# Masked query features written by four exponentials with their own bias columns

## What is computed

```python
h = _layernorm(x) * (1 + ca) + sa
x = x + ga * forward(h, ...)        # 3 layers, 16 heads of 8 channels
# in each layer
q, k, v = (out @ W + b  for Wq, Wk, Wv), split into heads
u = einsum(x * dh**-0.25, omega);  hh = 0.5 * sum(xs * xs)
favor(x) = concatenate([exp(u - hh), exp(-u - hh)]) * m**-0.5      # m = 8 features a head
a = causal_linear_attention(favor(q), favor(k), v) @ Wo + bo
h = layer_norm(out + a)
out = layer_norm(h + relu(h @ W1 + bf1) @ W2 + bf2)
```

## Time and profile before

| | us |
|---|---|
| median of 3 runs | 1801.07 |
| lowest and highest of them | 1798.61, 1804.36 |
| span of the profiled execution | 1828.0 |
| TensorE busy in it | 1571.7 |
| VectorE busy in it | 1443.5 |
| ScalarE busy in it | 935.3 |
| GpSimd busy in it | 698.6 |

### The profile page before, as it was taken

How to read it: one execution, slowest core, us unless ns; L and a number is a source line. 1 busy time by engine, 2 the same in 40 slices (tenths; PEclk the granted TensorE clock), 3 DMA queues, 4 the chain that set the end, 5 groups by cost and what they waited for, 6 DMA issues and landing times.

```text
span 1828.0 us, 65037 instructions
## 1 busy us (share of the span) xinstructions
PE 1571.7 (86%) x27934; PEld 1150.5 (63%) x27934; DVE 1443.5 (79%) x3906; ACT 935.3 (51%) x1958; POOL 698.6 (38%) x620
## 2 busy tenths in 40 slices
PE   6777365399969999999999999999999999999853
PEld 4344254399946677776667777666677667777542
DVE  4998566766658888888888888888888988888864
ACT  4887476366524444445544444554444544444373
POOL 0777636345513234215224323423321522431354
PEclk9888655599969999999999999999999999999876
DMA  9730012333200000000000000100000000000437
GB/s 264 145 100 1 21 50 90 97 102 101 83 13 14 3 9 9 15 3 14 15 3 13 16 3 8 20 3 9 9 15 3 14 15 3 11 6 3 109 102 233
DMA packets 88606, 79.69 MB, mean 44 GB/s; under 512 B 22416, under 2 KB 77040, under 8 KB 88064
## 3 DMA queue, kind: packets, MB, share of 16 engines
q1 hardware_dynamic: 70736, 46.17, 9.6%
q0 software_dynamic: 10848, 25.70, 4.9%
q10 hardware_dynamic: 6736, 3.66, 0.7%
HBM read 46.74 MB, written 34.01 MB: 44 GB/s over the span
## 4 chain that ended last, share of the span: by engine, by line
PE 50%; DVE 13%; ACT 4%; issue 2%; DMA 1%; DVEq 1%; POOL 0%; another core or an unknown queue 0%; POOLq 0%; ACTq 0%
PE psum L1965 8%; PE psum L1890 8%; PE psum L1859 4%; PE psum L1868 4%; PE psum L1928 2%; PE psum L1934 2%; PE psum L1882 2%; PE psum L1936 2%; PE psum L1875 2%; PE psum L1937 2%; PE psum L1938 2%; PE psum L1948 2%; PE psum L1847 2%; DVE at_kb L1543 2%; PE psum L1929 2%
## 5 line engine op out<-in xcount | busy, mean ns | idle before, releaser
L1890 PE MATMUL psum<-attn_w,at_qa 128*128 128x128 f32 x1536 | 197.6, 282 | 0.0
L1752 POOL TENSOR_TENSOR at_xres<-at_xn,attn_rows 128x512 f32<-128x512 f32 x32 | 40.9, 1277 | 394.2 <-DVE at_xn L368 394.2
L1965 PE MATMUL psum<-at_vT,attn_w 128*128 128x512 f32 x384 | 180.6, 614 | 6.8 <-ACT at_vT L1697 5.8
L1890 PEld LDWEIGHTS psum<-attn_w,at_qa 128*128 128x128 f32 x1536 | 179.6, 192 | 6.1 <-issue 0.7
L1543 DVE TENSOR_SCALAR at_kb<-at_kf,const 128x512 f32<-128x512 f32 x192 | 178.4, 989 | 0.0
L1757 POOL TENSOR_TENSOR at_xn<-at_sqk,attn_rows 128x512 f32<-128x512 f32 x48 | 63.6, 1326 | 202.8 <-DVE at_sqk L368 202.8
L1549 DVE STREAM_TRANSPOSE at_vb<-at_vT 32x512 uint32<-32x512 uint32 x192 | 134.7, 701 | 1.9
L1669 ACT ACTIVATE at_qa<-at_qf,const 128x512 f32<-128x512 f32 x192 | 127.6, 714 | 1.6
L1713 ACT ACTIVATE at_qa<-psum,attn_bf 128x512 f32<-128x512 f32 x192 | 122.1, 678 | 10.6 <-PE psum L1965 5.4
L1565 DVE TENSOR_TENSOR at_weights<-psum,const 128x1024 f32<-128x1024 f32 x96 | 115.6, 1204 | 11.3 <-PE psum L1859 11.3
L361 ACT ACTIVATE at_rstd<-at_mv,const 128x4 f32<-128x4 f32 x96 | 28.1, 292 | 184.3 <-DVE at_mv L349 184.2
(11 more groups left out here) (308 smaller groups left out, 3884.2 us busy)
## 6 DMA issues: line engine op xcount, KB each, us to landing
ex_rows<-sorted_x SPq DMA_DIRECT2D x71, 129.0 KB
ti_rows<-tile_rows SPq DMA_DIRECT2D x8, 640.0 KB
x<-in_L_attn_x SPq DMA_DIRECT2D x8, 512.0 KB, 7.3
tile_rows<-in_L_attn_x SPq DMA_DIRECT2D x8, 512.0 KB
x<-token_y POOLq DMA_DIRECT2D x8, 512.0 KB
tile_y<-ti_rows SPq DMA_DIRECT2D x16, 192.0 KB
out<-x ACTq DMA_DIRECT2D x12, 256.0 KB
expert_w<-in_L_ffn_w SPq DMA_DIRECT2D x1, 2048.0 KB, 14.2
```

Source lines behind the costliest of these rows:

```text
L1890: last = mm(bank(f.s, 1)[:, c * D:(c + 1) * D], hidden[f.s][:, t, c * P:(c + 1) * P], k.w2[:, f.l, t, :], start=(t == 0 and c == 0), stop= ...
L1965: mm(bank(f.s, c), k.w1[:, f.l, c * P:(c + 1) * P], hT[f.s][:], start=True, stop=True).then_inc(hid_ready, 1)
```

## The change

The four masked tiles are written by four exponentials straight from the PSUM bank, each with its own bias column `query_bias[:, l, i]`: for the partitions of its own heads the old bias, for the others the old form's zero is had as exp(x - 1e30). `qf` is no longer written by ScalarE; `queries_ready` is raised once a slot, after the fourth exponential, and all four stand ahead of the hidden activations. TensorE's fourth block and its scores both wait for that one. The wait for `outcome_free` moves to VectorE, before the last normalisation. The twelve bias columns are made once, by four more instructions of VectorE ahead of `wu_taken`.

```diff
+OFF = 1.0e30
...
+        other_heads, query_bias = m.sb("at_other_heads", [P, HQ]), m.sb("at_query_bias", [P, L, HQ])
...
                     if ends:
                         dve.wait_ge(res_rstd, f.count * 2 + 2)
+                        if f.turn > 1:
+                            dve.wait_ge(outcome_free, f.turn - 1)
                         normalise(nc, lambda c: res[f.s][:, c, :], mv[f.s], rstd[f.s], outcome[f.s]).then_inc(last_ready, 1)
...
-                nc.vector.tensor_scalar(feature_bias[:].rearrange("p i l -> p (i l)"), bank(1, 0)[:, 0:2 * L], LN_FEATURE, None, ALU.add).then_inc(wu_taken, 1)
+                st.done(nc.vector.tensor_scalar(feature_bias[:].rearrange("p i l -> p (i l)"), bank(1, 0)[:, 0:2 * L], LN_FEATURE, None, ALU.add))
+                st.done(nc.vector.tensor_scalar(other_heads[:], cst(k, "mask_a"), -1.0, OFF, ALU.add, ALU.mult))
+                for l in range(L):
+                    biased = nc.vector.scalar_tensor_tensor(query_bias[:, l, :], cst(k, "mask_a"), feature_bias[:, 0, l:l + 1], other_heads[:], ALU.mult, ALU.add)
+                biased.then_inc(wu_taken, 1)
...
-                def masked_queries(s, half):
-                    for i in (2 * half, 2 * half + 1):
-                        last = nc.scalar.activation(qa[s][:, :, i, :], qf[s][:].rearrange("p (j i) -> p j i", i=SUB), ACT.Copy,
-                                                    scale=cst(k, "mask_a")[:, i:i + 1])
+                def masked_queries(s, l):
+                    for i in range(HQ):
+                        last = nc.scalar.activation(qa[s][:, :, i, :], bank(1 - s, 3).rearrange("p (j i) -> p j i", i=SUB), ACT.Exp,
+                                                    bias=query_bias[:, l, i:i + 1])
                     return last
...
                         act.wait_ge(feat_ready, n * 2 + 2)
-                        if l == 0 and a.before:
-                            act.wait_ge(outcome_free, a.turn - 1)
-                        nc.scalar.activation(qf[s][:], bank(1 - s, 3), ACT.Exp, bias=feature_bias[:, 0, l:l + 1]).then_inc(queries_ready, 1)
-                    if a:
-                        act.wait_ge(queries_ready, n * 2 + 1)
-                        masked_queries(s, 0)
+                        masked_queries(s, l).then_inc(queries_ready, 1)
...
                     if a:
-                        masked_queries(s, 1).then_inc(queries_ready, 1)
...
                             if a and c == 3:
-                                pe.wait_ge(queries_ready, n * 2 + 1)
+                                pe.wait_ge(queries_ready, n + 1)
...
-                        pe.wait_ge(queries_ready, n * 2 + 2)
+                        pe.wait_ge(queries_ready, n + 1)
```

## The result

The changed kernel takes 1802.35 us, the median of 20 runs (1799.91 to 1809.05). The kernel before, now with 20 runs as well, takes 1799.38 (1794.90 to 1804.36). The ratio is 1.0018 with a 95% interval of 1.0011 to 1.0026: some 3 us slower (2.0 to 4.7 by the interval), less than the 0.3% named as the bound, and of the size and sign that were forecast (+3.1). The forecast of 1804.2 was built on the median of three runs, 1801.07; with 20 runs the kernel before stands 1.7 us lower, which is most of the distance from 1804.2 to 1802.35. The two profiled executions can't be set against each other whole: after's span is 1807.2 us, before's 1828.0, and TensorE reaches the first matmul of the attention stage at 487.9 us in one and 509.7 in the other, before anything that was changed. So what follows compares distances within the attention stage.

The account below looks back on a forecast made before the run. TensorE's order of work was taken to bound the kernel, with ScalarE half idle. 48 slots at 0 plus 3.1 us at the start, on the median of 1801.07, gave 1804.2 us, range 1798 to 1812.7.

Parts of the forecast that it names:

- the 0.3% named as the bound: Whole kernel: a measurement tells about 0.3%, 5.4 us, from no change.
- The bound: Attention slots: TensorE's order of work sets the pace of 24.8 us a slot; ScalarE is half idle.
- Part 1: ScalarE in each of 48 slots: 0.82 us less work, 39 us in all, costed at nothing.
- Part 2: TensorE's fourth hidden block: waits for four exponentials; load at 2.50 to 2.68 us, free until 2.73, so no delay.
- the first rival: Fourth block's wait: exponentials 0.71 us apart hold it 0.18 us in 47 slots, 8.5 us, total 1812.7; chance 0.17.
- What I said would be absent: TensorE's wait list: no row for L1965, the hidden blocks' matmuls, on ScalarE's exponential.
- Part 3: Hidden activations behind four exponentials: start at 2.36 to 2.60 us in place of 1.95, cost nothing.
- Part 4: VectorE before the last normalisation: the wait for outcome_free moves there, cost nothing.
- Part 5: Stage start: GpSimd's products hold the new VectorE instructions; TensorE starts 3.1 us later, range 0.7 to 3.1, passed to the end.
- The second, ScalarE's relief: All slots: ScalarE's saved time is passed on, 39 us gained, total 1765; chance 0.03.

Follow-up runs that it names:

- the delays: Changed kernel with an extra exponential of 32, 256 or 512 elements ahead of the four: ratios to the kernel before 1.0024, 1.0042 and 1.0083.
- the moved sums in the kernel before: Kernel before, with all four parts of the state sums ahead of TensorE's first feed-forward product and nothing else: ratio 0.9990 (0.9974 to 1.0007).

## Why the prediction was right

- The bound. That TensorE's order sets the pace, and ScalarE's busy time doesn't, held: 44.6 us of ScalarE work gone gave nothing, 63 us added behind the activations cost nothing. What counts is when a ScalarE result comes that TensorE waits for, as the delays and the moved sums in the kernel before show.
- Part 1. 39 us less of ScalarE's work was forecast from the lengths of the rows, 44.6 us were measured over the whole kernel. The four exponentials have 115.9 us of busy time where the exponential and the copies had 32.6 and 127.6, since their rows overlap; the activations fell from 122.1 to 117.8 for the same reason. None of it reached the time.
- Part 2. The exponentials follow each other at (2.41 - 0.69) / 3 = 0.57 us, closer than the 0.59 to 0.65 taken from the neighbours, and the load came at 2.47 where 2.50 to 2.68 was forecast. The 0.65 was a misreading that the trace of before can settle:

```profile
1106.42 0.67 ACT L1713 ACTIVATE at_qa<-psum,attn_bf 128x512 f32<-128x512 f32 x1
...
1107.79 0.69 ACT L1713 ACTIVATE at_qa<-psum,attn_bf 128x512 f32<-128x512 f32 x1
```

These are the second and the fourth activation of the earlier trace rows, whose first starts at 1105.85. The second starts 0.57 later, the third another 0.57, and only the fourth 0.80: it waits for TensorE's fourth block, whose half matmuls end at 1107.75. So L1713 had shown the 0.57 already, and the first rival, which lived on a slack of 0.05 us, was less likely than the 0.17 it was given. The step that carried part 2, that a load costs nothing until 2.73, was worked out from one exposed load; the delays on either side of it bear it out. What I said would be absent isn't quite: the view of L1677 has TensorE's weight loads waiting for it, 47 times and 14.1 us in all. All of that is hidden behind matmuls.

- Part 3. The activations started at 2.28 and took 2.45, a little ahead of the 2.36 to 2.60 forecast, so the cover held.
- Part 4. VectorE has no wait on GpSimd in the attention stage.
- Part 5. 3.1 us was the forecast for the release, 2.9 the measurement, by the mechanism named: one instruction held to the end of GpSimd's first product, the next to that of the second. What the step missed is that VectorE's own chain carries the columns as well, so an earlier release alone brings nothing. Its last claim, that the 3.1 us pass to the end, isn't borne out in full: in the trace 2.1 of the 2.9 us are left at the second slot (37.2 to 39.3 us from the first clearing of the carries); the first scores took 3.38 us in the changed kernel and 3.69 before, and there was a wait of 0.64 for "issue" in before. That the measured 3.0 us meet the forecast 3.1 so closely is in part luck: the start accounts for some 2 us of them, and where the rest comes from isn't known. The traces can't tell it: from the first slot's first matmul with xT to the last slot's it took 1167.8 to 1172.6 us in the traces with the changed slots that have no delay, and 1169.1 and 1170.3 in the two with the slots of before.
- The rivals. The first one, exponentials too far apart, was the right one to fear in kind: its price per us is what the series shows, and the kernel stood 0.26 us away from it. Its 0.18 us took the last exponential at 0.71; with 0.68, as in the sum of part 2, it is 3 x 0.71 + 0.68 + 0.05 - 2.73 = 0.13 us, 6.1 us in place of 8.5. The second, ScalarE's relief, gave nothing alone, and 0.8% with TensorE's order changed.

## What to carry to other kernels

Work taken off an engine beside the path is worth nothing until the bounding engine's order is changed to use it; try the change and the reordering together, since either alone can measure as nothing. At a wait, work out how late it may end for nothing (the hidden load, here 0.33 us beyond its old place) before counting what it got longer by. Put small VectorE instructions that read and write SBUF, one input or two, where GpSimd is idle, and look for the second chain before moving a release forward. A number that agrees is no proof of its cause: only a run that takes the cause away shows how much of the loss was its own.

## What the runs showed of the hardware

- Four-element VectorE instructions took 1.26 and 1.30 us beside a GpSimd product of 512 elements and 0.17 without, the one with one tensor input (L1612) like the one with two (L1614), and GpSimd's second product got its turn between them. VectorE's memset of 2304 elements (L1592 of before) wasn't held: 1.98 us beside both products (from 520.85) and 1.98 with GpSimd idle (from 525.40).
- Four ScalarE instructions of 512 elements from PSUM on end start 0.57 us apart, though the profile gives each 0.69 to 0.72 us: their rows overlap by 0.12 to 0.15 us. The hidden activations have rows of 678 ns before (L1713) and 724 ns after (L1716) for the same work, and start 0.57 us apart in both where none waits, so a row's length isn't the price in a sequence.
- An fp32 weight load that isn't hidden costs 0.10 us of TensorE's time at a granted clock of 1.00, though its own row is 0.19 us long.
